# Graph layer on one core: a fourth pair of row tiles transposed by DMA, with loads, weights and PSUM banks put in another order

## What is computed

```python
h = relu(layernorm(x))                              # called h0 below
type_sum = adj @ h
attn_a = sigmoid(concat([type_sum, h]) @ Wa.T + ba)
attn_b = sigmoid(concat([type_sum, h]) @ Wb.T + bb)
hw = h @ W_sa
s = (hw @ a_left)[:, None] + (hw @ a_right)[None, :]
e = where(adj != 0, exp(-leaky_relu(s, 0.01)), 0)
x_a = (e / (sum(e, 1) + 1e-5)) @ hw
x_b = adj @ (h @ W_gcnb) + b_gcnb
out = x + sigmoid(attn_a * x_a + attn_b * x_b)
```

## Time and profile before

| | us |
|---|---|
| median of 3 runs (lowest, highest) | 177.54 (177.13, 178.27) |
| execution with the profile: time | 176.94 |
| its span | 175.1 |
| PE busy | 170.5 (97%) |
| DVE busy | 144.5 (83%) |
| ACT busy | 113.2 (65%) |
| POOL busy | 24.5 (14%) |

### The profile page before, as it was taken

How to read it: one execution, slowest core, us unless ns; L and a number is a source line. 1 busy time by engine, 2 the same in 40 slices (tenths; PEclk the granted TensorE clock), 3 DMA queues, 4 the chain that set the end, 5 groups by cost and what they waited for, 6 DMA issues and landing times.

```text
span 175.1 us, 3378 instructions
## 1 busy us (share of the span) xinstructions
PE 170.5 (97%) x1313; PEld 124.6 (71%) x1313; DVE 144.5 (83%) x306; ACT 113.2 (65%) x167; POOL 24.5 (14%) x43
## 2 busy tenths in 40 slices
PE   7999999999999999999999999999999999999992
PEld 2556764455554478888744488888888888888892
DVE  3799995589999995999999703999999999976551
ACT  3769996349868889298658600875875874863310
POOL 4846441002007930000000000000000000000000
PEclk9999999999999999999999999999999999999998
DMA  5999999986999369900010100000010010011101
GB/s 135 296 213 260 226 231 175 207 157 110 215 220 332 146 112 216 247 28 2 0 64 0 60 0 0 4 0 0 4 60 0 6 60 0 4 62 60 64 30 30
DMA packets 9071, 17.66 MB, mean 101 GB/s; under 512 B 3920, under 2 KB 4704, under 8 KB 8288
## 3 DMA queue, kind: packets, MB, share of 16 engines
q0 software_dynamic: 1728, 8.39, 25.0%
q1 hardware_dynamic: 7328, 9.06, 16.3%
HBM read 22.94 MB, written 2.11 MB: 143 GB/s over the span
## 4 chain that ended last, share of the span: by engine, by line
PE 97%; DVE 1%; issue 0%; ACT 0%; DVEq 0%
PE ps L822 32%; PE ps L865 16%; PE ps L863 16%; PE ps L864 16%; PE ps L856 6%; PE ps L797 6%; PE ps L905 3%; PE ps L791 1%; PE ps L926 0%; DVE logit L771 0%; DVE e_lo L557 0%; PE ps L818 0%; ACT logit L434 0%; DVE res L664 0%; DVE e_hi L519 0%
## 5 line engine op out<-in xcount | busy, mean ns | idle before, releaser
L863 PE MATMUL ps<-mv_lo,e_hi 128*128 128x257 f16 (+2 forms) x272 | 71.0, 267 | 0.0
L865 PE MATMUL ps<-mv_hi,e_lo 128*128 128x257 f16 (+2 forms) x272 | 70.9, 266 | 0.0
L864 PE MATMUL ps<-mv_hi,e_hi 128*128 128x257 f16 (+2 forms) x272 | 70.8, 266 | 0.0
L400 ACT ACTIVATE z<-z,log_e 128x1024 f32<-128x1024 f32 x32 | 36.7, 1146 | 31.2 <-DVE z L601 31.2
L601 DVE SCALAR_TENSOR_TENSOR z<-sl_row,exs,far 128x512 f32<-128x512 f32 x64 | 45.1, 746 | 0.6 <-DMA sl_row<-sl_line 0.6
L609 DVE TENSOR_TENSOR e_lo<-z,e_hi 128x1024 f16<-128x1024 f32 x32 | 39.0, 1220 | 1.4 <-ACT e_hi L410 1.4
L822 PE MATMUL ps<-adj,nat_lo 128*128 128x512 f16 x128 | 36.8, 379 | 0.0
L822 PE MATMUL ps<-adj,nat_hi 128*128 128x512 f16 x128 | 36.7, 379 | 0.0
L410 ACT ACTIVATE e_hi<-z 128x1024 f16<-128x1024 f32 x32 | 33.3, 1041 | 0.0
L863 PEld LDWEIGHTS ps<-mv_lo,e_hi 128*128 128x128 f16 x272 | 26.4, 97 | 3.4 <-ACT c_sb L388 0.3
L864 PEld LDWEIGHTS ps<-mv_hi,e_hi 128*128 128x128 f16 x272 | 26.5, 98 | 3.1
(11 more groups left out here) (69 smaller groups left out, 170.0 us busy)
## 6 DMA issues: line engine op xcount, KB each, us to landing
adj<-in_adj_t POOLq DMA_DIRECT2D x6, 1024.0 KB, 9.8
x_sb<-in_x SPq DMA_DIRECT2D x6, 512.0 KB, 8.2
out<-res SPq DMA_DIRECT2D x7, 256.0 KB, 2.0
adj<-in_adj_t POOLq DMA_DIRECT2D x4, 256.0 KB, 6.7
adj<-in_adj_t POOLq DMA_DIRECT2D x2, 512.0 KB, 8.7
x_sb<-in_x SPq DMA_DIRECT2D x3, 256.0 KB, 4.0
sl_row<-sl_line SPq DMA_DIRECT2D x2, 256.0 KB, 5.5
sl_row<-sl_line SPq DMA_DIRECT2D x1, 512.0 KB, 7.0
```

Source lines behind the costliest of these rows:

```text
L400: act.activation(z[:, n % ZRING, :, :], z[:, n % ZRING, :, :], ACT.Exp, bias=log_e[:, 0:1], scale=SLOPE - 1.0).then_inc(exp_done, 1)
L863: pe.matmul(ps[:, bank, cols], e_hi[:, s, i1], mv_lo[:, j, cols], start=(j == 0), stop=False)
L864: pe.matmul(ps[:, bank, cols], e_hi[:, s, i1], mv_hi[:, j, cols], start=False, stop=False)
L865: return pe.matmul(ps[:, bank, cols], e_lo[:, s, i1], mv_hi[:, j, cols], start=False, stop=(j == NT - 1))
```

## The change

- LATE is 4: pair 4 (tiles 8 and 9) is transposed by DMA as well, and unit 5 no longer by PE. wide(5) moves from the early part to behind b_products(1, 0, 5); wide(6), wide(7), wide(8) stand behind j = 8, 11 and 15.
- WIDE_BANKS: pairs 4 to 7 use banks 0, 4, 2, 0 in place of 6, 2, 0, 2 (each the first of two), with waits on mv_ready and agg_ready ahead of them. The scores-line parts use banks 6, 1, 2. Its second part is transposed after b_pair(5), and copied by ACT after nat_highs(7).
- Piece (1, 0, 8) of the adjacency is split in two. Both halves are issued by POOL behind norms(6) and a wait for sl_moved 1; then norms(7), norms(8), piece (1, 8, 16), a wait for its landing, and piece (2, 0, 8); (2, 8, 16) follows behind the wait for all transposes.
- SP issues the transposes of pair 4 between the store and the spread of the first scores line, and no longer waits for the last piece of chunk 0. The last weights wg and the rows of biases are loaded only when (2, 0, 8) has landed; their cast moves to n = 8 (ACT) and n = 9 (DVE).
- narrow_results(4) moves to n = 1, mv_highs(4) to n = 1 and mv_lows(4) to n = 2 of the loops. DVE's early order is written out, with moments(7) and moments(8) earlier.

```diff
--- before.py
+++ after.py
@@ -52,17 +52,17 @@
 UNITS = ((0, 1), (1, 2), (2, 4), (4, 6), (6, 8), (8, 10), (10, 12), (12, 14), (14, 16))
 NU = len(UNITS)
 SL_PARTS = ((0, 4), (4, 8), (8, 16))
-SL_UNITS = (3, 5)
-SL_BANKS = (6, 6, 0)
+SL_UNIT = 3
+SL_BANKS = (6, 1, 2)
 SL_COLS = slice(BANK - P, BANK)
 X_PARTS = ((0, 1), (1, 2), (2, 4), (4, 6), (6, 8), (8, 12), (12, 16))
 
-LATE = 3
+LATE = 4
 ONTIME = NPAIR - LATE
 NTURN = NU - LATE
-WIDE_BANKS = (6, 2, 6, 2, 6, 2, 0, 2)
+WIDE_BANKS = (6, 2, 6, 2, 0, 4, 2, 0)
 B_BANKS = (4, 6, 4, 4)
-ADJ_PIECES = ((0, 0, 2), (0, 2, 4), (0, 4, 6), (0, 6, 8), (0, 8, 12), (0, 12, 16), (1, 0, 8), (1, 8, 16), (2, 0, 8), (2, 8, 16), (3, 0, 8), (3, 8, 16))
+ADJ_PIECES = ((0, 0, 2), (0, 2, 4), (0, 4, 6), (0, 6, 8), (0, 8, 12), (0, 12, 16), (1, 0, 4), (1, 4, 8), (1, 8, 16), (2, 0, 8), (2, 8, 16), (3, 0, 8), (3, 8, 16))
 
 
 def x_part(u):
@@ -250,9 +250,6 @@
             load_x(5)
             sp.wait_ge(adj_landed[1], 16)
             load_x(6)
-            sp.wait_ge(x_landed[6], 16)
-            sp.dma_start(wg_sb[:, :, :], w_post).then_inc(wg_landed, 16)
-            sp.dma_start(r_sb[:, :], rows).then_inc(rows_landed, 16)
             def sl_store(h):
                 lo, hi = SL_PARTS[h]
                 sp.wait_ge(sl_moved, h + 1)
@@ -272,14 +269,15 @@
                                  transpose=True).then_inc(h0t_landed[p - ONTIME], 16)
 
             sl_store(0)
+            turn_by_dma(4)
             sl_spread(0)
-            sp.wait_ge(adj_landed[piece_of(0, NT - 1)], 16)
-            turn_by_dma(ONTIME)
-            turn_by_dma(ONTIME + 1)
+            for p in range(5, NPAIR):
+                turn_by_dma(p)
             sl_store(1)
-            turn_by_dma(ONTIME + 2)
             sl_spread(1)
             sp.wait_ge(adj_landed[piece_of(2, 0)], 16)
+            sp.dma_start(wg_sb[:, :, :], w_post).then_inc(wg_landed, 16)
+            sp.dma_start(r_sb[:, :], rows).then_inc(rows_landed, 16)
             sp.wait_ge(turned, NTURN)
             sp.wait_ge(nat_ready, NPAIR)
             for g in range(NG):
@@ -329,15 +327,18 @@
             norms(4)
             load_adj(5)
             norms(5)
+            norms(6)
+            pool.wait_ge(sl_moved, 1)
             load_adj(6)
-            norms(6)
+            load_adj(7)
             norms(7)
             norms(8)
-            load_adj(7)
+            load_adj(8)
+            pool.wait_ge(adj_landed[8], 16)
+            load_adj(9)
             for p in range(ONTIME, NPAIR):
                 pool.wait_ge(h0t_landed[p - ONTIME], 32)
-            load_adj(8)
-            load_adj(9)
+            load_adj(10)
             pool.wait_ge(scales_ready, NPAIR)
             pool.tensor_scalar(column[:, :], scale_a[:, :], PROD, None, ALU.mult).then_inc(column_done, 1)
             pool.wait_ge(column_done, 1)
@@ -352,8 +353,8 @@
             ins.then_inc(narrow_ready, 1)
             pool.wait_ge(b_done, 1)
             pool.wait_ge(far_ready, JP)
-            load_adj(10)
             load_adj(11)
+            load_adj(12)
 
         @block.scalar
         def _(act):
@@ -374,8 +375,8 @@
 
             def mv_highs(p):
                 act.wait_ge(exs_ready, p + 1)
-                if p + 1 in SL_UNITS:
-                    sl_lines(SL_UNITS.index(p + 1))
+                if p + 1 == SL_UNIT:
+                    sl_lines(0)
                 act.activation(scale_a[:, 2 * p:2 * p + 2], exs[:, 2 * p:2 * p + 2, SR], ACT.Exp, bias=log_s[:, 0:1],
                                scale=-SLOPE).then_inc(scales_ready, 1)
                 act.wait_ge(scales_ready, p + 1)
@@ -446,23 +447,25 @@
             h0_tiles(3)
             mv_highs(0)
             nat_highs(2)
-            for p in range(1, NPAIR):
+            for p in range(1, 3):
                 if p + 2 < NTURN:
                     h0t_highs(p + 2)
-                if p + 2 < NPAIR:
-                    h0_tiles(p + 3)
-                    nat_highs(p + 2)
-                if p < ONTIME - 1:
-                    mv_highs(p)
-            mv_highs(ONTIME - 1)
+                h0_tiles(p + 3)
+                nat_highs(p + 2)
+                mv_highs(p)
+            for p in range(5, NPAIR):
+                h0_tiles(p + 1)
+                nat_highs(p)
+            sl_lines(1)
+            mv_highs(3)
             agg_highs(0)
-            act.wait_ge(wg_landed, 16)
-            act.activation(wg_hi[:, :, :], wg_sb[:, :, :], ACT.Copy, scale=W_SCALE).then_inc(wg_high, 1)
 
             for n in range(NE):
                 act_exp(n)
                 if n >= 1:
                     act_high(n - 1)
+                if n == 1:
+                    mv_highs(4)
                 if n == 2:
                     mv_highs(5)
                 if n == 3:
@@ -474,6 +477,8 @@
                     agg_highs(1)
                 if n == 8:
                     sl_lines(2)
+                    act.wait_ge(wg_landed, 16)
+                    act.activation(wg_hi[:, :, :], wg_sb[:, :, :], ACT.Copy, scale=W_SCALE).then_inc(wg_high, 1)
                 if n in (8, 9, 11, 12):
                     half_added((8, 9, 11, 12).index(n))
                 if n == 10:
@@ -682,22 +687,25 @@
             h0t_lows(2)
             moments(4)
             mv_lows(0)
-            for p in range(1, ONTIME - 1):
-                nat_lows(p + 1)
-                if p > 1:
-                    mv_lows(p - 1)
-                moments(p + 4)
-                narrow_results(p)
-                h0t_lows(p + 2)
-            moments(NU - 1)
-            nat_lows(ONTIME)
-            mv_lows(ONTIME - 2)
-            narrow_results(ONTIME - 1)
-            for p in range(ONTIME + 1, NPAIR):
-                nat_lows(p)
-            mv_lows(ONTIME - 1)
+            nat_lows(2)
+            moments(5)
+            narrow_results(1)
+            h0t_lows(3)
+            nat_lows(3)
+            mv_lows(1)
+            moments(6)
+            narrow_results(2)
+            h0t_lows(4)
+            moments(7)
+            nat_lows(4)
+            mv_lows(2)
+            moments(8)
+            narrow_results(3)
+            nat_lows(5)
+            nat_lows(6)
+            nat_lows(7)
+            mv_lows(3)
             agg_lows(0)
-            w_post_low()
             dve_far(0)
             for n in range(NE):
                 if n + 1 < NE:
@@ -705,7 +713,10 @@
                 dve_z(n)
                 if n >= LAG:
                     dve_low(n - LAG)
+                if n == 1:
+                    narrow_results(4)
                 if n == 2:
+                    mv_lows(4)
                     narrow_results(5)
                 if n == 3:
                     mv_lows(5)
@@ -718,6 +729,8 @@
                     mv_lows(7)
                 if n == 8:
                     agg_lows(1)
+                if n == 9:
+                    w_post_low()
                 if n == 10:
                     b_parts(0)
                     agg_lows(2)
@@ -806,10 +819,10 @@
                 if u == 1:
                     pe.wait_ge(wa_ready, 1)
                 for t in range(*UNITS[u]):
-                    if t >= 4:
+                    if 4 <= t < 8:
                         pe.wait_ge(mv_ready, t - 3)
-                    if u in SL_UNITS and t == UNITS[u][0]:
-                        sl_lines(SL_UNITS.index(u))
+                    if t == UNITS[SL_UNIT][0]:
+                        sl_lines(0)
                     wide_part(t, slice(0, WA)).then_inc(wide_product, 1)
 
             def sl_lines(h):
@@ -834,9 +847,11 @@
 
             def b_products(c, j0, j1):
                 if j0 == 0 and c == 1:
-                    pe.wait_ge(mv_ready, 2 * ONTIME)
+                    pe.wait_ge(mv_ready, 6)
+                    pe.wait_ge(sl_moved, 1)
                 if j0 == 0 and c >= 2:
                     pe.wait_ge(agg_ready, 1 if c == 2 else 3)
+                    pe.wait_ge(mv_ready, 12)
                 for j in range(j0, j1):
                     pe.wait_ge(adj_landed[piece_of(c, j)], 16)
                     b_half(c, j, 0)
@@ -940,14 +955,24 @@
                     turn(p + 2)
                 if p + 1 < NTURN:
                     wide(p + 1)
-            b_products(1, 0, 8)
+                if p == 5:
+                    pe.wait_ge(h0t_ready, 4)
+                    sl_lines(1)
+            b_products(1, 0, 5)
+            pe.wait_ge(h0t_ready, NTURN)
+            pe.wait_ge(sl_moved, 2)
+            wide(5)
+            b_products(1, 5, 9)
+            pe.wait_ge(agg_ready, 1)
             wide(6)
-            b_products(1, 8, 12)
-            pe.wait_ge(h0t_ready, NTURN)
+            b_products(1, 9, 12)
+            pe.wait_ge(mv_ready, 8)
             wide(7)
             b_products(1, 12, 16)
+            pe.wait_ge(mv_ready, 10)
             wide(8)
             b_products(2, 0, 10)
+            pe.wait_ge(mv_ready, 14)
             sl_lines(2)
             b_products(2, 10, 16)
             a_pair(0)

```

## The result

The changed kernel takes 185.39 us (median of 6 runs, 181.53 to 188.93); the kernel before, on the same chip, 177.31 us. Medians are of all runs, ratios of the fast runs alone, those within 1.5% of their kernel's fastest (here 181.53, 182.41 and 183.72). The ratio is 1.0295, 95% interval 1.0222 to 1.0368: slower by about 3%. Forecast was 177.4, range 176.6 to 179.2. The profiled execution took 183.72 us with a span of 181.9, against 176.94 and 175.1. What follows explains those 6.8 us of span.

What follows compares the result with a forecast made beforehand. PE, busy 97% of the span, was taken to bound the kernel. Removed transposes (-0.43 us) and a wait ahead of A (+0.31 us) summed to -0.1 us: 177.4 us, range 176.6 to 179.2.

Steps and rivals of the forecast that it cites:

- The adjacency: Loads of chunks 1 and 2 on q0 land before PE needs them: cost nothing, bounds 0 to 1 us.
- rival 1: At wide(5) and wide(6), transposes starved by the loads: +1.1 to +3.2 us, middle 179.7 us; chance 0.22.
- 256 bytes or 4 KB a turn: Pair 4's transposes beside q0's loads: 4 KB turns land it by 28; 256-byte turns only when q0 is done.
- The scores line: Its broadcast lands so that z(0) on DVE starts at 34.4, range 33.5 to 35.6; before it was 35.40.
- A moving by z(0) - 34.5: A's start on PE moves by z(0)'s start minus 34.5, at best -0.43 us: -0.43 to +1.1 us.
- from z(0) to the copy 28.13 us: Chain from z(0) on DVE to ACT's scores-line copy ahead of A: 27.26 us plus 0.87 added, 28.13 us.
- PE's work: PE loses only the transposes of unit 5, all on the path: gain at best 0.43 us.

Runs made afterwards that it cites:

- held apart: Changed kernel with transposes of pairs 5 to 7 waiting until load (1, 8-16) has landed, and chunk 2's loads waiting for them: 188.08 us, ratio 1.0590.
- other order: Changed kernel with scores line's store and broadcast, then all eight transposes, (1, 8-16) ahead of norms(8), chunk 2 behind the transposes, wide products later: 182.50 us.
- small kernel: Separate kernels computing none of the output, with loads beside transposes or plain copies; in the longer overlap the second load took 13.4 us beside transposes, 14.2 beside copies.
- pair 4 alone: Changed kernel with only pair 4 transposed by DMA and pairs 5 to 7 copied plainly: 177.63 us, ratio 0.9985.
- late weights alone: Kernel before with only the last weights and bias rows loaded behind (2, 0-8), their casts at n = 8 and 9: 177.24 us, ratio 0.9990.
- smaller packets: Changed kernel with loads (1, 8-16) and (2, 0-8) each cut into two halves, packets of 4096 bytes: 182.56 us, ratio 1.0282.

## Why the prediction was wrong

**The step that failed** is "The adjacency ... Cost nothing; bounds 0 to 1 us". It had (1, 8-16) land at 33 to 34.5, with 3 us of room. It landed at 42.52. Two things are in that. The smaller is seen with copies in place of transposes: the load took 11.0 us and would have landed near 36.2, with 1.1 us of room, 1.7 to 3.2 later than forecast. The rate of the earlier trace rows, 0.20 MB/us, held there while q0 ran (0.62 MB from 32 to 35), but q0 didn't run all the time: from 20.5 to 23 us it started 58 packets of 4096 bytes, where from 24 on it started about 25 in half a microsecond, and from 29 to 30.5 us it started 3. From the end of the load's last packet (36.4) to the landing passed 0.3 us. That alone would have cost nothing. The larger, 6.3 us, comes only with the transposes, and had no term in the sum.

**What the transposes do was asked from one side only.** The prediction asked whether the loads would starve the transposes (rival 1, 0.22) and never whether the transposes would hold back the loads. Rival 1 named wide(5) and wide(6). wide(5) never waited. At wide(6) the mechanism was there but hidden: pair 5's low half, issued at 25.95, landed 17.0 us later, at 43.0; without the stall wide(6) would have wanted it at 38.2. The chain shows the first wait; behind it stood a second. In both experiments that moved the first one PE waited for a transposed pair: at wide(6) when held apart, at wide(5) in the other order.

**256 bytes or 4 KB a turn.** I took turns of 4 KB. From 32 to 35 us both queues started 73 packets each, and in the small kernel 98 of q1 to 117 of q0: as many of the one as of the other, which is the reading of one 256-byte packet a turn that I set aside. The rule of the Trainium skill (DMA: Bandwidth & Descriptors, Queues, rings and completion order) of typically 9 to 17 descriptors in a turn doesn't describe these queues, if the trace's 256 bytes are descriptors. Pair 4 was in time all the same (29.4 and 30.1) since q0 had pauses: of the 1024 packets of its two transposes 451 started between 25 and 26 us and 402 between 28.5 and 30, as the loads (1, 0-4) and (1, 4-8) came to their ends (landed 26.1 and 29.7), and only 122 in the 2.5 us between. So it landed when q0 let it, as rival 1 had it, but q0 let it earlier than the 33.4 of that rival. (Rival 1's second wait is 2.1 us by its own numbers, 41.8 - 39.7, and not 2.3.)

**The scores line.** z(0) was put at 34.4, range 33.5 to 35.6; it began at 35.79. In the changed kernel that was hidden by the stall: by the prediction's own rule, A moving by z(0) - 34.5, A would have begun 1.3 us later than before with no stall at all, so this term too was sized too low (forecast -0.1). The rule "from z(0) to the copy 28.13 us" held: with copies z(0) began at 35.20 and ACT's copy ended at 63.23, 28.03 later, and A waited 0.55. Where z(0) came at 32.38, A began at 62.41.

**PE's work.** Forecast at best -0.43; A came 0.36 us earlier with pair 4 alone. The steps at 20.72, 29.07 and 33.39 were forecast at 20.88, 29.24 and 33.6. This part was right. What the change is worth when nothing stands still is no more than that: 0.9964 of the time before in the kernel with plain copies, 0.9985 with pair 4 alone.

**The clock** was not in the sum. A wait of 5 us cost 7.4: 5.24 and 2.15 at the half clock behind it. The half clock also stood behind the waits of 2.51 and 3.74 us (held apart) and 2.77 (other order), and not behind the one of 1.59. Rival 1, with its two waits, should have had this on top.

Most of the cause is settled: transposes against copies (185.39 and 176.66), and pairs 5 to 7 against pair 4 (187.61 and 177.63). What makes packets stand still together is open. The loss needs the transposes; that transposes beside large loads don't suffice is shown by the small kernels and, inside the layer, by the late weights alone, where pairs 5 and 6 ran beside the same load; and 4 KB packets don't prevent it. One difference was left untested: with the late weights alone the broadcast of the scores line had landed at 28.8, ahead of the transposes, while in the five profiles in which the load took over 14 us it was issued before pair 5 and landed at 32.0 to 39.2. In the kernel before it landed at 35.4 beside a load that took 8.8, but there it was issued behind that load, so neither the broadcast nor its order is shown to be the trigger. Pair 4 alone may not be quite free of it: five of its ten runs were 178.36 us or more (three of 17 of the kernel before, the highest 178.81), though the ratio shows no difference, and its profile, a run of 176.54, holds no packet. None of the four versions measured here with four pairs transposed by DMA beats the kernel before.

## What to carry to other kernels

Before DMA transposes are moved beside loads with a deadline, give the load a term of its own: here the same load took 11.0 us beside plain copies and, in three profiles, 16.8 to 17.9 beside transposes, but 11.0 beside transposes in another arrangement, so it has to be measured in place. Ask of any two transfers put together what each does to the other, and look for the second deadline behind the first. A saving of 0.4 us on an engine that is 97% busy is not worth moving 1 MB loads to within 1 us of their use, as one stall costs its length and then the clock.

## What was unexpected of the hardware

- Packets of both queues, 4-byte ones included, stood for 2 to 8 us and many were let go at one moment (37.48 and 38.74 with pairs 5 to 7 transposed; 30.8 with smaller packets). The changed kernel's DMA carried 60 GB/s from 35 to 40 us, against 213 in the 5 us before. At least one packet of over 2 us stands in every profile with all four pairs transposed, also where only pair 4 was in flight (in the kernel that held the other pairs back, packets that began at 26.1 to 26.9 ended between 28.2 and 29.2). Without transposes beside it the longest was 2.19 us, of a load beside plain copies.
- Behind such a hold, 76 of 80 packets of 256 bytes took about 635 or 1250 ns instead of 18 to 31 (39 to 42 us), until the load's last packet was through at 42.16.
- SP's issue of a transpose of 128 KB took 1.2 to 1.3 us with no load in flight and up to 7.6 us beside loads. That is no mark of transposes: a plain copy took 0.6 us and up to 6.7 beside loads in the kernel with pair 4 alone, and up to 8.6 in a small kernel.
- PE was granted half its clock (1.2 of 2.4 GHz) while and after standing 5 us: 0.52 from 40 to 45, 0.80 from 45 to 50.
